# Row scores of a two-layer graph network: three bf16 parts split as columns, turned into rows by one bf16 product, and all four engine orders set anew

## The reference, cut to what matters

```python
h   = relu(layernorm(x))
Wh  = einsum('bnf,hfo->bhno', h, W_heads)                 # 4 heads, 256 -> 256
f1, f2 = Wh @ a[:, :256], Wh @ a[:, 256:]                 # one number per node and head
e   = where(adj > 0, leaky(f1[..., :, None] + f2[..., None, :], 0.01), -1e9)
h2  = elu(softmax(e) @ Wh)                                # heads side by side: 1024 wide
Wh2 = h2 @ W_out; g1, g2 = Wh2 @ a_out[:256], Wh2 @ a_out[256:]
e2  = where(adj > 0, leaky(g1[:, None] + g2[None, :], 0.01), -1e9)
o   = elu(softmax(e2) @ Wh2)
x2  = x + layernorm(relu(o @ w1 + b1) @ w2 + b2 + o) * gamma + beta
h3  = relu(layernorm(x2))
out = x2 + deg * (h3 @ Wi.T + b) + adj @ (h3 @ Wj.T)
```

## Time and profile before

| what | value |
|---|---|
| median of 3 runs | 908.99 us |
| the profiled execution's own time | 909.05 us |
| its span, first to last instruction | 907.2 us |
| TensorE busy (matmuls) | 836.8 us, 92% |
| VectorE busy | 757.1 us, 83% |
| GpSimd busy | 703.9 us, 78% |
| ScalarE busy | 683.0 us, 75% |
| mean granted TensorE clock | 0.989 of full speed |

### The profile page before, as it was taken

One profiled execution on the slowest core, in us unless ns is written; L12 is line 12 of the kernel. 1 busy time (PEld: TensorE's weight loads), 2 busy tenths in 40 slices (PEclk: granted clock), 3 DMA queues, 4 the chain that ended last, 5 costly groups with the idle time before them and its releaser, 6 DMA issues.

```text
span 907.2 us, 20067 instructions
## 1 busy us (share of the span) xinstructions
PE 836.8 (92%) x6281; PEld 776.6 (86%) x6281; DVE 757.1 (83%) x1998; ACT 683.0 (75%) x1801; POOL 703.9 (78%) x948
## 2 busy tenths in 40 slices
PE   2699999999999999999999999999999999999964
PEld 1589989889998988999898899889889998989952
DVE  4978888898888889888888988888899888897753
ACT  3788878787777878778787877778777877877541
POOL 3587988877788887778888777888877788888852
PEclk9999999999999999999999999999999999999987
DMA  8100010111111011111101111110111111000000
GB/s 246 59 1 24 25 36 2 36 36 36 35 37 35 1 36 36 36 36 36 34 4 36 36 36 36 36 35 3 35 37 36 36 37 35 2 24 25 25 24 23
DMA packets 30136, 31.50 MB, mean 35 GB/s; under 512 B 1856, under 2 KB 28992, under 8 KB 30032
## 3 DMA queue, kind: packets, MB, share of 16 engines
q1 hardware_dynamic: 29776, 29.63, 10.5%
q0 software_dynamic: 256, 0.59, 0.3%
HBM read 21.82 MB, written 8.39 MB: 33 GB/s over the span
## 4 chain that ended last, share of the span: by engine, by line
PE 66%; DVE 17%; issue 9%; POOL 3%; ACT 2%; DMA 1%; SPq 0%; DVEq 0%; POOLq 0%; ACTq 0%
PE ps L1201 59%; DVE g_parts L598 4%; PE ps L1319 3%; DVE wo L711 2%; DVE lend L737 2%; PE ps L1275 2%; PE ps L1393 2%; DVE mj_lo L768 1%; DMA lend<-in_L_gnn_a_heads 1%; ACT mj_hi L1086 1%; DVE c_st L568 1%; DVE g_rest L589 1%; DVE g_parts L621 1%; DVE f_rep L669 1%; PE ps L1341 1%
## 5 line engine op out<-in xcount | busy, mean ns | idle before, releaser
L363 POOL TENSOR_TENSOR h_lo<-h2v,h_hi 128x512 fp32r<-128x512 f32 x128 | 166.6, 1302 | 0.1
L1201 PE MATMUL ps<-gh_hi,wh_hi 128*128 128x256 f32 x512 | 153.7, 300 | 1.6 <-DVE h2v L641 1.1
L1201 PE MATMUL ps<-wo_hi,h_hi 128*128 128x258 f32 x512 | 150.6, 294 | 0.0
L1201 PE MATMUL ps<-wo_lo,h_hi 128*128 128x258 f32 x512 | 145.1, 283 | 0.0
L1201 PE MATMUL ps<-wo_hi,h_lo 128*128 128x258 f32 x512 | 145.0, 283 | 0.0
L1201 PE MATMUL ps<-gh_lo,wh_hi 128*128 128x256 f32 x512 | 142.9, 279 | 0.0
L1201 PE MATMUL ps<-gh_hi,wh_lo 128*128 128x256 f32 x512 | 142.7, 279 | 0.0
L369 POOL TENSOR_SCALAR h2e<-h2e 128x512 f32<-128x512 f32 x128 | 86.2, 681 | 32.0 <-ACT h2e L959 31.8
L1201 PEld LDWEIGHTS ps<-wo_lo,h_hi 128*128 128x128 f32 x512 | 97.4, 190 | 4.3
L1201 PEld LDWEIGHTS ps<-wo_hi,h_hi 128*128 128x128 f32 x512 | 96.8, 189 | 4.6 <-POOL h_lo L363 0.4
L970 ACT ACTIVATE lend<-lend,zm 128x128 f32<-128x128 f32 x256 | 99.1, 393 | 0.0
(11 more groups left out here) (166 smaller groups left out, 2794.3 us busy)
## 6 DMA issues: line engine op xcount, KB each, us to landing
xa<-in_x SPq DMA_DIRECT2D x32, 256.0 KB, 3.1
xr<-in_x SPq DMA_DIRECT2D x32, 256.0 KB, 3.0
out<-res SPq DMA_DIRECT2D x32, 256.0 KB, 2.2
lend<-in_L_gnn_W_heads SPq DMA_DIRECT2D x4, 256.0 KB, 5.7
lend<-in_L_gnn_a_heads SPq DMA_DIRECT2D x4, 256.0 KB, 8.4
wo<-in_L_gnn_W_out SPq DMA_DIRECT2D x1, 1024.0 KB, 11.2
l1w_sb<-in_L_gnn_W SPq DMA_DIRECT2D x1, 512.0 KB, 9.7
lend<-in_L_gnn_w SPq DMA_DIRECT2D x2, 256.0 KB, 3.0
```

The costliest lines, as they stand in the source:

```text
L363: pool.tensor_tensor(h2_lo[:, u, :, :].rearrange("p c n -> p (c n)"), h2v[u % 2][:, :], h2_hi[:, u, :, :].rearrange("p c n -> p (c n)").bi ...
L1201: return pe.matmul(out_, lhs, rhs, start=start, stop=stop)
```

## The change

1. **The split comes ahead of the transpose.** `split_cols` takes the score columns where the products left them, in PSUM (16 columns in the first layer, 4 in the second), and splits them there in five VectorE instructions: a copy of the whole columns to SBUF for f1 and g1 (`f_cols`, `g_cols`), the first part, the rest written back to PSUM, the second part, the third part. Each of the last three waits for the one before. The parts go side by side into `f_split` or `g_split`, 48 columns of bf16.
2. **One bf16 product turns them into rows.** `score_rows` and `score_rows2` multiply the 48 columns with a bf16 identity and give 48 rows. One cast brings them to SBUF: ScalarE's `rows_copy` for the first layer, VectorE's `rows2_copy` for the second. `rowsel` has 48 partitions instead of 128.
3. **The order of each engine's step is written anew**, with another number of steps between some producers and consumers; the PSUM banks and the waits for them are set to match. SyncE's order stays.

```diff
-G3 = (32, 64, 96)
+COLS = 4 * H
+ROWS = 3 * COLS
...
-B_ROWS = 5
+B_ROWS = 7
-B_ROWS2 = 7
-B_SCORES2 = 6
+B_ROWS2 = 4
+B_SCORES2 = 7
...
-            def less_first(name, p, psum, parts, rest):
-            def second(name, p, parts, rest):
-            def third(name, p, parts, rest):
-            def f_cols(p):
-            def f_less_first(p):
-            def f_second(p):
-            def f_third(p):
-            def g_first(p):
-            def g_less_first(p):
-            def g_second(p):
-            def g_third(p):
+            def split_cols(name, p, cols, whole, parts):
+
+                dve.tensor_copy(whole, cols).then_inc(S[name[0]], 1)
+                dve.tensor_copy(parts[0], cols).then_inc(S[name[1] + "_first"], 1)
+                wait(dve, name[0], p)
+                wait(dve, name[1] + "_first", p)
+                dve.tensor_tensor(cols, cols, parts[0], ALU.subtract).then_inc(S[name[1] + "_rest"], 1)
+                wait(dve, name[1] + "_rest", p)
+                dve.tensor_copy(parts[1], cols).then_inc(S[name[1] + "_second"], 1)
+                wait(dve, name[1] + "_second", p)
+                dve.tensor_tensor(parts[2], cols, parts[1], ALU.subtract).then_inc(S[name[1] + "_third"], 1)
+
+            def f_cols_split(p):
                 wait(dve, "cols_done", p)
                 wait(dve, "rows_done", p, lag=1)
+                split_cols(("cols_copied", "rows"), p, ps[:, B_COLS, 0:COLS], f_cols[p.e][:, :],
+                           [f_split[p.e][:, k, :] for k in range(3)])
+
+            def wh2_scores(p):
+                wait(dve, "wh2_copied", p)
+                wait(dve, "rows2_done", p, lag=1)
+                split_cols(("wh2_scores_copied", "rows2"), p, ps[:, B_WH2[0]:B_WH2[0] + 2, F:WO], g_cols[p.e][:, :, :],
+                           [g_split[p.e][:, k, 0:4].rearrange("p (b j) -> p b j", b=2) for k in range(3)])
+
+            def rows2_copy(p):
                 wait(dve, "rows2_done", p)
                 wait(dve, "scores2_done", p, lag=2)
+                dve.tensor_copy(g_parts[p.e][:, :], ps[0:ROWS, B_ROWS2, 0:P]).then_inc(S["rows2_copied"], 1)
...
-            def f_first(p):
+            def rows_copy(p):
                 wait(act, "rows_done", p)
                 wait(act, "scores_done", p, lag=1)
-                act.activation(f_parts[p.e][:, :], ps[:, B_ROWS, 0:P], ACT.Copy).then_inc(S["rows_first"], 1)
+                act.activation(f_parts[p.e][:, :], ps[0:ROWS, B_ROWS, 0:P], ACT.Copy).then_inc(S["rows_copied"], 1)
...
             def score_rows(p):
-                wait(pe, "cols_copied", p)
-                wait_bank(p, ("cols_copied", 1, 0))
-                pe.transpose(ps[:, B_ROWS, 0:P], f_rep[p.e][:, :], ident[:, :]).then_inc(S["rows_done"], 1)
+                wait(pe, "rows_third", p)
+                wait_bank(p, ("scores2_masked", 1, 3), ("hidden_full", 2, 4), ("mj_lo", 1, 6), ("scores_masked", 1, 1))
+                mm(ps[0:ROWS, B_ROWS, 0:P], f_split[p.e][:, :, :].rearrange("p k r -> p (k r)"), ident_bf[:, :], True, True).then_inc(S["rows_done"], 1)
...
             def score_rows2(p):
-                wait(pe, "wh2_scores_copied", p)
-                pe.transpose(ps[:, B_ROWS2, 0:P], f2_rep[p.e][:, :], ident[:, :]).then_inc(S["rows2_done"], 1)
+                wait(pe, "rows2_third", p)
+                mm(ps[0:ROWS, B_ROWS2, 0:P], g_split[p.e][:, :, :].rearrange("p k r -> p (k r)"), ident_bf[:, :], True, True).then_inc(S["rows2_done"], 1)
...
             def scores2(p):
-                wait(pe, "rows2_third", p)
+                wait(pe, "rows2_copied", p)
...
             def one(pairs):
+                if p := pairs[4]:
+                    scores2(p)
+                if p := pairs[3]:
+                    h2_unit(p, 1, 1)
+                if p := pairs[2]:
+                    prob_transposes(p, 0)
+                if p := pairs[1]:
+                    score_rows(p)
```

More of the change, by code:

```diff
@@ L440, in one @@
             def one(pairs):
[L441 to L474, removed]
                 if p := pairs[3]:
                     elu_less(p, 2)
+                    h2_low(p, 1)
                     elu_less(p, 3)
-                    h2_low(p, 1)
+                if p := pairs[0]:
+                    rstd1(p)
                 if p := pairs[5]:
@@ L861, in one @@
                 if p := pairs[5]:
-                    out_elu(p)
+                    soft2(p)
+                if p := pairs[4]:
+                    elu(p, 2)
                 if p := pairs[3]:
-                    gh_low(p, 1)
+                    at_low(p, 1)
+                if p := pairs[6]:
+                    norm2_stats(p)
+                    norm2_var(p)
+                if p := pairs[4]:
+                    elu(p, 3)
+                if p := pairs[7]:
+                    add_mi(p, 0)
                 if p := pairs[2]:
                     score_mask(p, 1)
-                if (p := pairs[2]) and p.is_first():
-                    out_dots(0)
+                if (p := pairs[1]) and p.is_first():
+                    heads_dots(3)
+                if p := pairs[3]:
+                    gh_low(p, 0)
+                if p := pairs[7]:
+                    mj_low(p, 0)
                 if p := pairs[2]:
                     soft_max(p, 0)
+                if p := pairs[5]:
+                    out_elu(p)
                 if p := pairs[7]:
@@ L1421, in one @@
             def one(pairs):
+                if p := pairs[3]:
+                    gh_unit(p, 3)
+                if (p := pairs[1]) and p.is_first():
+                    adj_transpose()
+                if p := pairs[4]:
+                    wh2_part(p, 0, 3)
+                    wh2_part(p, 1, 3)
+                if p := pairs[5]:
+                    hidden(p, 0)
+                if (p := pairs[2]) and p.is_first():
+                    l1w_transposes()
+                if p := pairs[5]:
+                    hidden(p, 1)
@@ new lines, in one @@
+                if p := pairs[1]:
+                    score_cols(p)
+                if p := pairs[3]:
+                    h2_unit(p, 0, 0)
+                if p := pairs[4]:
+                    score_rows2(p)
+                if p := pairs[3]:
+                    h2_unit(p, 0, 1)
+                if p := pairs[5]:
+                    ffn_out(p)
+                if p := pairs[3]:
+                    h2_unit(p, 1, 0)
+                if p := pairs[6]:
+                    h3_transposes(p)
@@ L1422, in one @@
                 if p := pairs[1]:
                     scores(p, 0)
+                if p := pairs[3]:
+                    h2_unit(p, 3, 0)
+                    h2_unit(p, 3, 1)
+                    wh2_part(p, 0, 0)
+                if p := pairs[6]:
+                    mixed(p, 0)
+                if p := pairs[3]:
+                    wh2_part(p, 1, 0)
+                if p := pairs[1]:
+                    scores(p, 1)
                 if p := pairs[4]:
                     prob_transposes2(p)
+                if p := pairs[2]:
+                    gh_unit(p, 0)
```

472 lines of the change are left out of this document (203 added, 269 removed).

## The result

The changed kernel takes 919.35 us (median of 4, 918.27 to 921.02), against 909.62 us for the kernel before (median of 4, 908.40 to 910.56): a ratio of 1.011, 95% interval 1.009 to 1.013. I had forecast 887 with a range of 880 to 899. So the change is slower, by 10 us, and 32 us above the forecast.

The account below looks back on a forecast made before the run. TensorE, 92% busy, was taken as the bound, with one recurring wait at line 598. 909.05 - 25.5 (wait) + 3.2 (TensorE's own work) + 0 (ramps) = 886.75, so 887 us; range 880 to 899.

Parts of the forecast that it names:

- The bound and the wait that goes: TensorE bounds the kernel; its wait for line 598, second layer's third score part, stretched beside GpSimd, goes whole: -25.5 us.
- The price of a split: Five VectorE instructions reading PSUM take about 0.9 us per split, unstretched by GpSimd, and hide behind TensorE's work.
- What TensorE's own work costs: Two bf16 products replace two transposes (-0.11 us per pair), gaps add 0.27; sum +0.10 per pair, +3.2 us in all.
- The gap behind bf16: On TensorE, the first wide float32 matmul behind bf16 takes 0.09 us more; 4 such gaps per pair instead of 1.
- The ramps: Start and end of the pipeline: latency stays six steps, so 0 us, with 3 us either way.
- Rival (a): Short TensorE waits return, tightest at `score_rows` for the mask; `soft2` and `residual2` blocked 1.1 us each; 898 us, chance 0.19.
- Rival (b): `gather` becomes TensorE's new wait, for `mj_low`, if ScalarE comes late to `mj_high`; 920 us, chance 0.08.
- My signs: Right if once-per-pair matmul spacing is 25.4 to 25.6 us, TensorE waits stay under 0.1 us per step, splits are unstretched.

Follow-up runs that it names:

- third_early: The kernel before, with the third part of the second layer's scores computed right behind the second part, ahead of `hidden_whole`: 887.41 us, ratio 0.977.
- pad_both: The changed kernel with its 48 weight columns and 48 rows padded to 128 by zeros, instructions and order kept: 883.25 us, ratio 0.972.

## Why the prediction was wrong, step by step

**The bound and the wait that goes: right.** Line 598's collision was the one wait, and it went (one wait of 0.8 us is left where 24.7 us were). `third_early` shows its worth: 22 us, where my term was 25.5, and new waits of 3.7 us are about the difference. My period of 26.20 us was an average that took in two steps of 23 us at the ends of the stretch (82.1 to 105.2 and 818.5 to 841.9); a step between them is 26.47 us, 25.59 of it TensorE's own work. The sum took off the waits as a total, so this did not move it.

**The price of a split: right.** I had 0.9 us; the two splits take 0.86 us (first start 508.86, end 509.72) and 0.96 us (509.78 to 510.74). None is stretched by GpSimd, as the kin rows said and as follows from the Trainium skill ("SBUF — State Buffer", Who interferes with whom), by which a VectorE instruction with at most one SBUF input does not contend with GpSimd: `h_lo` ran on GpSimd from 508.11 to 509.39.

**What TensorE's own work costs: wrong, and this is the step that failed.** The prediction said that the narrower weights "cost and bring nothing", and priced a product with 48 rows by rows of products with 128. No row of the kernel before had a matmul with fewer than 128 partitions and 128 columns of weights, so this was an operation without a row. It should have been bounded from both sides, and was taken as free in one sentence. It costs 0.22 to 0.25 us at each of five places, 1.18 us per step: my +0.10 us per step became +1.1 us (26.68 against 25.59), and 887 + 32 x 1.0 = 919 us is what was measured. The Trainium skill's sentence on mode changes, cited above, stands on a page that I had not weighed; it would have made a rival that forecasts a slower kernel.

**The gap behind bf16: wrong in size, and small.** I had four gaps of 0.09 us. In `pad_both` the lone row product costs 0.12 us in all (0.36 less twice 0.12), as much as the transpose that it replaces (0.35 from 501.82 to 502.17), with its gap in it. The wide matmul behind takes 0.20 us after the bf16 product (514.12 to 514.32) and after the transpose alike (501.97 to 502.17): I charged the gap to one side only. Counted over one step, ten wide matmuls (256 columns or more) stand behind a short one in `pad_both` and nine in the kernel before, where I had three more. So the +3.2 us of this term did not come. With the operands filled TensorE's own step is 25.39 us, 0.20 below that of the kernel before; the part of this that the missing gaps do not explain is not traced. This is why the padded kernels end at 881 to 883 and not at 887.

**The ramps: right** within the 3 us given, by TensorE's waits: 24.8 us up to 100 us, against 26.9 before, and 16.1 us from 820 us on, against 16.6.

**Rival (a): the blocking came, the wait did not.** `soft2` and `residual2` are stretched in the median by 1.1 and 0.6 us, where row 737 had made it 1.1 each. VectorE carried it, and the slacks held: between 82 and 845 us the mask was never waited for. In `pad_both`, with the same order and a shorter step, `soft2` is back at 0.414 us in the median: the order alone does not decide it.

**Rival (b), the right number for the wrong reason.** It gave 920 us by a wait for `mj_lo`. There is none between 82 and 845 us: ScalarE's `mj_high` starts at 502.37, 0.2 us behind the end of the last product's place, as punctual as the forecast needed.

**My signs.** The spacing of the once-per-step matmul told it at once (26.68 instead of 25.4 to 25.6). The signs by waits and by medians all said "right". The busy share of TensorE is no sign: it is 95% in the changed kernel and in `pad_both` alike. The busy time is one: 872.5 us against 835.3 us in `pad_both` and 836.8 us before, with the same 6281 instructions.

## What to carry to other kernels

Here, between wide float32 matmuls, one to four bf16 matmuls with 48 or 64 partitions or columns of weights cost some 0.24 us of TensorE more than with 80 to 128. Where TensorE is the bound, fill such operands with zeros to 80 or more; here that cost one memset. Narrower operands than 48, and other types, were not run. An operation of a shape that the trace does not hold has no price from rows of another shape: bound it, and let it be a rival. When the waits vanish and the time does not, look at the distances between starts of the engine that is "busy", and try the smallest edit against a wait first: here moving one call got 22 us.

## What was not expected of the hardware

- The step between 64 and 80: 913.6, 882.4, 881.3 and 883.3 us with 64, 80, 96 and 128; 919.35 with 48. It holds for the partitions of the weights and for their columns: at 64 all five places cost what they cost at 48, and at 80 none does.
- The price is at the change, ahead and behind, and inside a row of narrow matmuls too: four take 0.32 instead of 0.21 us.
- None of it is shown as idle time of TensorE's matmuls; their busy time grew by 36 us with the same 6281 instructions.
- VectorE subtractions that write their result back to PSUM are hardly slower than the same that write to SBUF: 0.171 against 0.161 us for 4 columns, 0.183 against 0.174 us for 16.
